# A fused attention and low-rank FFN kernel: v projected with tokens on partitions, for two pairs of heads together

## The reference, cut to what matters

```python
x = x + _layernorm(_L0_attn_ref(_layernorm(x), Wq, Wk, Wv, Wo))       # x: (4, 512, 1024) f32
x = x + _layernorm(_L0_ffn_ref(_layernorm(x), A, B, Wr, br))

def _L0_attn_ref(h, Wq, Wk, Wv, Wo):                                  # 16 heads of 64, W*: (1024, 1024)
    q, k, v = h @ Wq, h @ Wk, h @ Wv
    q, k = rotary(q), rotary(k)
    logits = where(causal, q @ k.T, -1e9) / sqrt(64)
    return (softmax(logits) @ v) @ Wo

def _L0_ffn_ref(x, A, B, Wr, br):                                     # 8 experts of rank 16
    scores = 8 * softmax(x @ Wr.T + br)
    return 2 * einsum('bshr,hor,bsh->bso', einsum('bsd,hrd->bshr', x, A), B, scores)
```

## Time and profile before

| | |
|---|---|
| median of 3 runs | 1061.01 us (1060.8 to 1061.26) |
| the profiled execution | 1061.09 us |
| its span (first to last instruction) | 1059.3 us |
| PE busy, matmuls | 1041.6 us (98%) |
| DVE, ACT, POOL busy | 759.6, 638.5, 415.6 us (72%, 60%, 39%) |
| costliest PE lines: projections L1477, three forms | 325.9 + 304.4 + 302.8 us, 776 matmuls each |
| scores L1408, 256 columns and others | 100.1 us, 384 matmuls |
| transposes of probabilities L1508 | 111.6 us, 640 |
| chain that ended last, share of L1477, L1408, L1508, L1450 | 50%, 23%, 6%, 1% |

### The profile page before, as it was taken

How to read it: one execution, slowest core, us unless ns; L and a number is a source line. 1 busy time by engine, 2 the same in 40 slices (tenths; PEclk the granted TensorE clock), 3 DMA queues, 4 the chain that set the end, 5 groups by cost and what they waited for, 6 DMA issues and landing times.

```text
span 1059.3 us, 18177 instructions
## 1 busy us (share of the span) xinstructions
PE 1041.6 (98%) x5495; PEld 866.6 (82%) x5495; DVE 759.6 (72%) x2138; ACT 638.5 (60%) x1454; POOL 415.6 (39%) x422
## 2 busy tenths in 40 slices
PE   7999999999999999999999999999999999999996
PEld 6888888888888888888888888888887888888884
DVE  8677777786666767676676757676667777777777
ACT  6667777776665766666565756666685333333334
POOL 4153443434252544434352534434466232333221
PEclk9999999999999999999999999999999999999999
DMA  7122424242311346021111202021232323322311
GB/s 278 41 85 70 130 71 135 70 135 55 101 55 31 110 169 229 15 72 50 31 51 35 71 11 71 11 75 49 87 135 61 119 81 100 120 102 91 104 60 61
DMA packets 58695, 90.76 MB, mean 86 GB/s; under 512 B 3568, under 2 KB 36336, under 8 KB 58608
## 3 DMA queue, kind: packets, MB, share of 16 engines
q1 hardware_dynamic: 58464, 89.44, 25.9%
q10 hardware_dynamic: 144, 0.26, 0.1%
HBM read 64.52 MB, written 25.17 MB: 85 GB/s over the span
## 4 chain that ended last, share of the span: by engine, by line
PE 93%; DVE 2%; ACT 1%; issue 1%; POOL 1%; DVEq 0%; ACTq 0%; POOLq 0%
PE bank L1477 50%; PE bank L1408 23%; PE bank L1508 6%; PE bank L1527 3%; PE bank L1526 3%; PE bank L1642 2%; PE bank L1619 1%; PE bank L1450 1%; PE bank L1643 1%; PE bank L1529 1%; PE bank L1493 1%; PE bank L1438 1%; DVE stats L1187 1%; POOL big_lo L660 1%; PE bank L1420 0%
## 5 line engine op out<-in xcount | busy, mean ns | idle before, releaser
L1477 PE MATMUL bank<-big_hi,w_hi 128*128 128x512 f32 (+1 forms) x776 | 325.9, 420 | 0.3 <-DVE big_lo L1037 0.3
L597 POOL TENSOR_SCALAR prob<-prob,rinv 128x128 f32<-128x128 f32 (+3 forms) x256 | 136.3, 532 | 444.7 <-DVE rinv L1072 444.6
L1477 PE MATMUL bank<-big_hi,w_lo 128*128 128x512 f32 (+1 forms) x776 | 304.4, 392 | 0.0
L1477 PE MATMUL bank<-big_lo,w_hi 128*128 128x512 f32 (+1 forms) x776 | 302.8, 390 | 0.0
L742 ACT ACTIVATE prob<-prob,nmax 128x128 f32<-128x128 f32 (+3 forms) x256 | 144.0, 562 | 215.9 <-DVE nmax L1062 214.3
L1477 PEld LDWEIGHTS bank<-big_hi,w_lo 128*128 128x128 f32 x776 | 145.6, 188 | 32.8
L1477 PEld LDWEIGHTS bank<-big_hi,w_hi 128*128 128x128 f32 x776 | 146.5, 189 | 19.7 <-issue 0.4
L1477 PEld LDWEIGHTS bank<-big_lo,w_hi 128*128 128x128 f32 x776 | 147.1, 190 | 11.5
L1062 DVE CUSTOM_DVE_ANT_0 prob<-bank,mask 128x256 f32<-128x256 f32 (+2 forms) x192 | 106.2, 553 | 37.1 <-PE bank L1408 31.9
L1080 DVE TENSOR_TENSOR pT_lo<-bank,pT_hi 128x128 fp32r<-128x128 f32 (+3 forms) x256 | 124.2, 485 | 2.6 <-ACT pT_hi L753 2.4
L1508 PE MATMUL bank<-ident,prob 128*128 128x128 f32 x640 | 111.6, 272 | 1.2 <-DVE pT_lo L1080 0.8
(11 more groups left out here) (148 smaller groups left out, 1893.6 us busy)
## 6 DMA issues: line engine op xcount, KB each, us to landing
w_raw<-in_wqkv SPq DMA_DIRECT2D x48, 512.0 KB, 4.9
attention_out<-o_sum SPq DMA_DIRECT2D x64, 128.0 KB, 2.3
w_raw<-attention_out SPq DMA_DIRECT2D x16, 512.0 KB, 4.9
land<-in_x SPq DMA_DIRECT2D x16, 512.0 KB, 3.6
out<-res SPq DMA_DIRECT2D x14, 512.0 KB, 2.6
xin<-in_x SPq DMA_DIRECT2D x12, 512.0 KB, 5.7
xT_hold_hi<-xin SPq DMA_DIRECT2D x8, 512.0 KB, 3.7
xT_hold_lo<-xn SPq DMA_DIRECT2D x8, 512.0 KB, 5.4
```

The costliest lines, as they stand in the source:

```text
L597: pool.tensor_scalar(p, p, rinv[:, q % 4:q % 4 + 1], 1.0, ALU.mult, ALU.mult).then_inc(prob_done, 1)
L1477: done = pe.matmul(grp_ps[(b + k) % 2][:, cols], w, xt[:, cols], start=at == 0, stop=at == GROUP_MM - 1)
```

## The change

v is no longer projected per unit with the weights stationary. A *group* g is four units (two pairs of heads x two batches). Job m (32 of them; `v_job`) takes group m // 4, one batch, and two token tiles of 128: the stationary operand is a 128x128 tile of the transposed x, and the moving one is the weight of v of both pairs, 2 x 128 = 256 columns. A job is 48 matmuls (2 tiles x 8 chunks x 3) of 256 columns, and its result has tokens on partitions, in one bank (`tr_ps`; job 0 in `o_ps`). `v_turn`, `v_raw` and the buffer `raw` are gone. Jobs 0 and 1 are both run in unit 0 (12 matmul places a step instead of 9, each place of a v job being two narrow matmuls), job u+1 in unit u up to 30, none in unit 31, where the remaining 48 matmuls are spread over steps 0 to 5 (8 a step).

A job is drained at step 0 of the next unit: ACT makes two high parts (`v_high(m, p)`, one per pair of heads, before the step's exponent) and DVE two low parts (`v_low(m, p)`, behind negate and pt_low). The first pair's v goes to `v_hl`; the second pair's into parts of the transposed probabilities that no matmul reads because of the causal mask (`v_pair`, `v_tile`), for which the high and low buffers become one, `pT`; `o_low` lies in such parts too. Attend of head 0 now waits for its job: of units 4g and 4g+2 for job 4g+1, of units 4g+1 and 4g+3 for job 4g+3.

v's weights have their own buffers (`wv_raw`, which shares memory with `wv_lo`, and `wv_hi`). For group g+1 they are loaded at the start of unit 4g+3 (once the last job of group g is summed), copied by ACT at steps 2 and 3 (`wv_high`) and subtracted by POOL at steps 3 and 4 (`wv_low`), and used from step 5 of the same unit. The q and k steps on POOL move from 2, 5 (sums) and 4, 7 (low parts) to 1, 6 and 5, 7. `HOLD_AT` moves from (4, 7) to (1, 3). Semaphore counts, the choice of banks and the buffers of the FFN's `bt` follow. The number of weight transfers stays; one more is at the start of the program, and one less later. The second half's x is needed from unit 15 (job 16).

```diff
-HOLD_AT = (4, 7)
+HOLD_AT = (1, 3)
+QUAD = 4
...
+        wv_hi = sb(ctx, "wv_hi", [P, 2, EMBED], F32R)
+        sV = ExitStack()
+        wv_raw = sb(sV, "wv_raw", [P, 2, EMBED])
+        sV.close()
+        wv_lo = sb(ctx, "wv_lo", [P, 2, EMBED], F32R)
...
+        sH = ExitStack()
+        holes = sb(sH, "holes", [P, 4, QT, SEQ])
+        sH.close()
+        pT = sb(sB, "pT", [P, 4, QT, SEQ], F32R)
+        pT_hi, pT_lo = pT[:, 0:2, :, :], pT[:, 2:4, :, :]
...
+        o_low = holes[0:DH, :, 1, 0:P]
...
+        def v_job(m):
+
+            return m // QUAD, m % QUAD // 2, 2 * (m % 2)
+
+        def v_bank(m):
+
+            return o_ps if m == 0 else tr_ps
+
+        def v_summed_in(u):
+
+            return [0, 1] if u == 0 else [u + 1] if u < UNITS - 1 else []
+
+        def v_read_in(u):
+
+            return [0, 1] if u == 1 else [u] if 2 <= u < UNITS else []
+
+        def v_pair(m, p, lo):
+
+            g, b, j = v_job(m)
+            d = slice(DH * lo, DH * lo + DH)
+            if p == 0:
+                return v_hl[:, b, j:j + 2, :, d]
+            if b == 0 and j == 0 and g % 2:
+                return pT[:, :, 3, 2 * P:3 * P].rearrange("p (t h) d -> p t h d", t=2)[:, :, :, d]
+            return pT[:, j:j + 2, 3 if b else 2, 0:2 * P].rearrange("p t (h d) -> p t h d", h=2)[:, :, :, d]
...
+        def v_tile(a, j, h):
+
+            g, p, b = a // QUAD, a % QUAD // 2, a % 2
+            if p == 0:
+                return v_hl[:, b, j, h, :]
+            if b == 0 and j < 2 and g % 2:
+                return pT[:, 2 * j + h, 3, 2 * P:3 * P]
+            return pT[:, j, 3 if b else 2, P * h:P * h + P]
...
+            def load_wv(g, p):
+
+                if g > 0:
+                    sp.wait_ge(v_sum_done, QUAD * g)
+                sp.dma_start(wv_raw[:, p, :], wqkv[2, (2 * g + p) % PAIRS, :, :]).then_inc(wv_in[p], 16)
...
+                if u % QUAD == QUAD - 1 and u < UNITS - 1:
+                    load_wv(u // QUAD + 1, 0)
+                    load_wv(u // QUAD + 1, 1)
...
-                    if s == 1 and b == 0 and real(u) and late(n, 1):
-                        w_low(2, n)
+                    if u % QUAD == QUAD - 1 and u < UNITS - 1 and s in (3, 4):
+                        wv_low(u // QUAD + 1, s - 3)
                     if b == 1 and not (isinstance(u, int) and u >= UNITS - 1):
-                        if s in (2, 5):
-                            w_pairs(s // 5, n + 1)
-                        if s in (4, 7):
+                        if s in (1, 6):
+                            w_pairs(s // 6, n + 1)
+                        if s in (5, 7):
...
-            def v_raw(u, b):
-                act.wait_ge(grp_done, 3 * u + 3)
-                act.activation(raw[:, :], grp_ps[b][:, :], ACT.Copy).then_inc(v_read, 1)
-
-            def v_high(u, b, fill):
-                act.wait_ge(tr_done, fill + 1)
-                if late(u, 2):
-                    act.wait_ge(pv_done, 2 * (u - 1))
-                act.activation(v_hl[:, b, :, :, 0:DH].rearrange("p j h d -> p (j h) d"),
-                               tr_ps[:, :].rearrange("p (j d) -> p j d", d=DH), ACT.Copy).then_inc(v_hi_done, 1)
+            def v_high(m, p):
+                act.wait_ge(v_sum_done, m + 1)
+                if m > 2:
+                    act.wait_ge(pv_done, 2 * (m - 2))
+                act.activation(v_pair(m, p, 0), v_sums(m, p), ACT.Copy).then_inc(v_hi_done, 1)
...
+                    if s == 0:
+                        for m in v_read_in(u):
+                            v_high(m, 0)
+                            v_high(m, 1)
                     exponent(u, s)
-                    if s == 0 and real(u - 1):
-                        v_raw(u - 1, 1 - b)
-                    if s == 2 and real(u - 1):
-                        v_high(u - 1, 1 - b, fill)
                     if prepares(u, ahead) and s == 6:
                         ln_start(ahead_tile(u) + 1)
                     pt_high(u, s)
...
@@ -821,15 +875,15 @@
                     if s == 5 and real(u - 2) and not (isinstance(u, int) and u > UNITS):
                         o_lower(u - 2, 1)
                     if real(u):
-                        if s == 0 and b == 0 and late(n, 1):
-                            w_high(2, n)
+                        if u % QUAD == QUAD - 1 and u < UNITS - 1 and s in (2, 3):
+                            wv_high(u // QUAD + 1, s - 2)
                         if s == 3:
                             q_high(u, b)
...
-            def v_low(u, b):
-                dve.wait_ge(v_hi_done, u + 1)
-                dve.tensor_tensor(v_hl[:, b, :, :, DH:2 * DH].rearrange("p j h d -> p (j h) d"),
-                                  tr_ps[:, :].rearrange("p (j d) -> p j d", d=DH),
-                                  v_hl[:, b, :, :, 0:DH].rearrange("p j h d -> p (j h) d").bitcast(F32),
-                                  ALU.subtract).then_inc(v_lo_done, 1)
+            def v_low(m, p):
+                dve.wait_ge(v_hi_done, 2 * m + 2)
+                dve.tensor_tensor(v_pair(m, p, 1), v_sums(m, p), v_pair(m, p, 0).bitcast(F32), ALU.subtract
+                                  ).then_inc(v_lo_done, 1)
...
                     if not closing or (u == UNITS and s == 0):
                         pt_low(u, s - 1)
+                    if s == 0:
+                        for m in v_read_in(u):
+                            v_low(m, 0)
+                            v_low(m, 1)
                     if s == 0 and real(u - 1):
...
+            def v_project(m, kept, first, count):
+
+                g, b, j0 = v_job(m)
+                for mm in range(2 * first, 2 * (first + count)):
+                    t, at = mm // GROUP_MM, mm % GROUP_MM
+                    c, part = (at // 2, at % 2) if at < 2 * KC else (at - 2 * KC, 2)
+                    if mm == 0:
+                        pe.wait_ge(wv_hi_done, 2 * g + 2)
+                        if m > 1:
+                            pe.wait_ge(v_hi_done, 2 * m)
+                            pe.wait_ge(v_lo_done, 2 * m)
+                        if kept:
+                            pe.wait_ge(tr_hi, kept)
+                            pe.wait_ge(tr_lo, kept)
+                    if mm == 2 * KC:
+                        pe.wait_ge(wv_lo_done, 2 * g + 2)
+                    if m == UPH and t == 0 and part == 0 and c % PART == 0:
+                        pe.wait_ge(xT_in[c // PART], 32)
+                    tile = slice(P * (j0 + t), P * (j0 + t) + P)
+                    x_t = (xT_lo if part == 1 else xT_hi)[:, b, c, tile]
+                    w = (wv_lo if part == 2 else wv_hi)[:, :, P * c:P * c + P]
+                    done = pe.matmul(v_bank(m)[:, 2 * P * t:2 * P * t + 2 * P].rearrange("p (a n) -> p a n", a=2), x_t, w,
+                                     start=at == 0, stop=at == GROUP_MM - 1)
+                if first + count == GROUP_MM:
+                    done.then_inc(v_sum_done, 1)
...
                     if h == 0:
-                        pe.wait_ge(v_hi_done, a + 1)
-                        pe.wait_ge(v_lo_done, a + 1)
+                        m = QUAD * (a // QUAD) + 2 * (a % 2) + 1
+                        pe.wait_ge(v_hi_done, 2 * m + 1 + a % QUAD // 2)
+                        pe.wait_ge(v_lo_done, 2 * m + 1 + a % QUAD // 2)
...
+                total = GROUP_MM * (2 + len(v_summed_in(u)))
+                third = 4 if u == 0 else 3
+                kept = x_count(u, half, ahead) + 2 if ahead else 0
+
+                def project_next(first, count):
+                    if real(u):
+                        for at in range(first, min(first + count, total)):
+                            if at < 2 * GROUP_MM:
+                                project(u, b, n, at, 1)
+                            else:
+                                v_project(v_summed_in(u)[at // GROUP_MM - 2], kept, at % GROUP_MM, 1)
+
                 for s in range(STEPS):
-                    third = MM_STEP // 3
-
-                    def project_third(k):
-                        if real(u):
-                            project(u, b, n, half, MM_STEP * s + third * k, third)
-
-                    project_third(0)
-                    if s == 2 and real(u - 1):
-                        v_turn(u - 1, x_count(u, half, ahead))
+                    per = 8 if u == UNITS - 1 else 3 * third
+                    project_next(per * s, third)
                     scores(u, s, b)
-                    project_third(1)
+                    project_next(per * s + third, third)
                     turn_probs(u, s)
-                    project_third(2)
+                    project_next(per * s + 2 * third, per - 2 * third)
```

156 lines of the change are left out of this document (71 added, 85 removed).

## The result

The changed kernel takes 1071.57 us (median of 4 runs, 1070.99 to 1072.55) against 1060.9 us for the kernel before in the same session: a ratio of 1.0101, 95% interval 1.0084 to 1.0119. The forecast was 1064.6 us with a range up to 1069.0: the direction was right, the size was not, and the time lies outside the range.

A forecast was written before the change was run, and what follows sets the result against it. PE's matmul stream was taken as the bound: -14.4 (transposes) + 6.4 (narrow matmuls) + 5.7 (attend waits) + 2.4 (weight waits) + 3.5 (ends) = +3.6 us on 1061.1; forecast 1064.6 us, range 1055.5 to 1069.

The forecast's parts named there:

- What bounds the kernel: Whole kernel: a stream of PE matmuls, PE busy 1041.6 of 1059.3 us and 93% of the chain.
- the plain stream: PE in all units: transposes of v gone, -14.4 us, narrow matmuls added, +6.4, a gain of 8.0 us.
- The second rival: v's projection: a 256-column matmul costs 0.115 us, the split adding 0 to 1.9: 1058.2 to 1060.1 us; chance 0.15.
- I take 0.35, so 7 units cost 2.4 us: Step 6 of units 3, 7, ... 27: PE waits 0 to 0.6 us for POOL's low part of v's weights.
- The attend wait: Step 0 of units 3, 7, ... 31: PE waits for DVE's v subtraction, 0.35 us in six units, 1.8 in two; 5.7.
- The ends: 24 matmuls move from unit 31 to unit 0: 5.5 us lost, 2 gained, so 3.5 given back; bounds 0 and 5.6.
- late x transfers and the end: Rival: unit 15's xT transfers land late and shorter unit 31 gains nothing: 3 to 5 us more, about 1069; chance 0.1.
- 12 ns: v's projection: the rows were said to show 12 ns more for the split than the skill's 2.5 ns gap rule.
- the last rival: All terms: losses a little smaller, waits of half size, 2.5 us given back at the end: 1060.7 us; chance 0.15.

The follow-up runs named there:

- the narrow form by itself: Kernel before, with each 512-column matmul of v's projection made as two of 256 columns: 1066.9 us, ratio 1.0053.
- the kernel with three edits: Changed kernel with v's low-part matmuls last in a job, v's high parts ahead of x normalisation (units 2, 6), attend's wait split: 1061.4 us, ratio 1.0004.
- the high parts first: Changed kernel, but in units 2 and 6 ACT makes v's two high parts ahead of the next x tile's normalisation: 1069.9 us, ratio 1.0084.
- the light copies: On the kernel with three edits, ACT's copies of chunks 2 to 5 of wo take 64 of 1024 columns: 1060.4 us, ratio 0.9994.
- k earlier: Unit 31 with 10 projection matmuls a step, k rotated and copied at step 5: 1076.4 us on the changed kernel, 1065.9 on the kernel with three edits.
- the low part last: Changed kernel, but a v job takes its 16 matmuls with the low part of v's weights after the 32 with the high part: 1067.7 us, ratio 1.0062.
- the last kernel: The kernel with three edits, plus half-chunk copy ahead of v's weights (units 3, 7) and unit 31's k head 1 and second attention-output high part later: 1059.1 us.

## Why the prediction was wrong

- **What bounds the kernel, and the plain stream.** Right. 8.0 predicted, 8.1 measured by distances; the narrow form by itself is 5.7 and not 6.4. The second rival (the split is free) is out.
- **"I take 0.35, so 7 units cost 2.4 us"** is the step that failed: 7.5 measured by distances, of which 0.5 is attend's restart. Its mechanism was right: POOL's second subtraction is late behind q's slow low part. In five units it was mis-sized: 0.60 of plain wait, which my own rows gave as the upper bound (for the 0.35 I had none), plus the restart (0.8 in all; 1.1 in unit 15, and why 0.3 more there was not tested). In units 3 and 7 a cause was missed: the half-chunk copy at its new step keeps ACT, DVE and POOL late (1.6 each). The run with the half-chunk copy ahead of v's weights shows that its place costs about 1 us for each of the two, on the kernel with three edits; for the changed kernel itself the rows of unit 3 show the chain, and no run has that edit alone.
- **The attend wait.** Place, releaser and the six late units right (0.27 each for 0.35, and 0.35 with the 0.08 of restart). For units 3 and 7 I took 1.8; it was 2.2. ACT's normalisation starts 0.41 us before the nominal time of attend (93.03 against 93.44), where I had it 0.92 before: with four transposes of x gone from the end of step 7, PE comes to attend 0.45 sooner, and ACT doesn't. That this is the reason is read from the rows and wasn't run. The run with the high parts first shows ACT's share: 0.9 each. The short waits in units 2 and 6, 1.1 together, I had put at nothing, again by looking only at the step that x's copy left.
- **The ends.** 3.5 predicted and measured; the 2 us taken for unit 31 was a guess between 0 and 5.5, so hitting it to 0.1 is luck. That ACT and POOL hold PE up there is borne out: the light copies give 1.0 and leave PE waiting for POOL. My attempt to mend it (k earlier) made it worse.
- **The range.** Its upper end took 3 to 5 us more from late x transfers and the end, neither of which happened in the changed kernel, and nothing from the seven waits together at their own upper bounds (0.6 each: 1.8 more), let alone from restart.
- **Slips of the working.** The "12 ns" a split goes with the pair of 0.1195 and 0.227; the 6.4 goes with 8, and 7.5 was measured. The 4 us of waits at attend in the last rival isn't half of 5.7 (2.85, which would give 1059.6).

What stays open: how the late units' 0.8 divides between DVE's slow low part of q (1.63 us beside POOL's subtraction, 0.69 undisturbed) and POOL's plain order. No kernel without that overlap was tried.

## What to carry to other kernels

When a step of preparation is moved, look at the step that it arrives in, on each engine that it uses, and not only at the one that it leaves. A wait on a saturated matmul stream costs more than the idle time shown: take the distance between starts, and count the restart. And a dependency that arrives late in the very step that needs it can be met on the consumer's side: reordering the products so that the late operand is used last, and splitting one wait into two, gave back more here (3.9 and 4.2) than earlier production did (1.6 and 2.3). One wait removed can also just lengthen the next, so such edits are judged together.

## What the runs showed of the hardware

**A stall can cost the clock as well.** In the profile of the low part last, PE waits 1.93 us at attend of unit 3, as in the changed kernel, but comes back at half speed: a matmul of 512 columns takes 0.42 to the next start (98.69 to 99.11) and not 0.23, and the granted clock of these 5 us is 0.66. Timeline of PE and, below it, the windows around it (us; busy of PE, PEld, DVE, ACT, POOL; granted clock, DMA share, GB/s):

```profile
95.62 0.71 PE L1597 MATMUL bank<-pT,v_hl 128*128 128x512 f32 x1 [1.93 <-DVE v_hl L1160]
96.12 0.63 PE L1598 MATMUL bank<-pT,v_hl 128*64 128x512 f32 x1
...
99.11 0.28 PE L1563 MATMUL bank<-k_all,q_hl 128*128 128x256 f32 x1
```

```profile
90.00:95.00 5.00, 3.69 (x21) 2.80 (x19) 3.54 (x14) 4.93 (x11) 0.59 (x1) 1.00 0.74 197
95.00:100.00 5.00, 4.38 (x16) 3.55 (x17) 1.84 (x5) 0.88 (x3) 0.69 (x1) 0.66 0.98 349
100.00:105.00 5.00, 5.00 (x30) 4.25 (x29) 3.09 (x10) 3.48 (x9) 2.82 (x4) 1.00 0.15 36
```

The changed kernel's own profile has a granted clock of 1.00 in the same 5 us. From the attend's first matmul to the first score takes 99.11 - 95.62 = 3.49 us, where the changed kernel, after a wait of 2.00, has 97.54 - 95.61 = 1.93: 1.56 us lost, with the clock at its lower level, 1.2 GHz, in part of the stretch. Whether a stall of this length drops the clock differs from run to run, and the mean granted clock of each run goes with its time. The two quicker runs of this kernel (1066.9 both) have 0.998, the two slower ones (1068.5 and 1069.4) 0.996. Of the last kernel's 11 runs the four quickest have 0.998 or more (1057.8 to 1058.5) and the rest 0.997. So the clock is a likely cause of the spread; where in a run it fell, only the profiled ones show.
